# Scores of a linear attention: two heads on the two row halves of the TensorE array, their stacks filled by transfers within SBUF

## The reference, cut to what matters

```python
q = (hidden_states @ Wq).reshape(b, l, h, f).transpose(0, 2, 1, 3)   # h = 16 heads, f = 16
k = (hidden_states @ Wk).reshape(b, l, h, f).transpose(0, 2, 1, 3)
v = (hidden_states @ Wv).reshape(b, l, h, hd).transpose(0, 2, 1, 3)  # hd = 8
q = q * f ** (-0.5)
...
A = jnp.einsum('bhcf,bhsf->bhcs', qi, ki) ** 2 * mask                # within a chunk of 64
o = (inter_o + intra_o) / (inter_z + intra_z + EPS)[..., None]       # inter: all earlier chunks
...
x = x + 0.5 * ffn(layernorm(x)); x = x + attn(layernorm(x)); x = x + 0.5 * ffn(layernorm(x))
```

## Time and profile before

| | before |
|---|---|
| median of 3 runs | 235.53 us (234.33 to 237.14) |
| span of the profiled execution | 232.5 us, 6133 instructions |
| PE busy, weight loads busy | 200.5 us (86%), 161.8 us (70%) |
| DVE, ACT, POOL busy | 156.7 us (67%), 150.9 us (65%), 79.2 us (34%) |
| chain that ended last | PE 51%, DVE 30%, ACT 6%, issue 5%, DMA 5%, SP's queue 1% |

### The profile page before, as it was taken

How to read it: one execution, slowest core, us unless ns; L and a number is a source line. 1 busy time by engine, 2 the same in 40 slices (tenths; PEclk the granted TensorE clock), 3 DMA queues, 4 the chain that set the end, 5 groups by cost and what they waited for, 6 DMA issues and landing times.

```text
span 232.5 us, 6133 instructions
## 1 busy us (share of the span) xinstructions
PE 200.5 (86%) x2375; PEld 161.8 (70%) x2375; DVE 156.7 (67%) x419; ACT 150.9 (65%) x346; POOL 79.2 (34%) x100
## 2 busy tenths in 40 slices
PE   7655877849999996996999999987898999999973
PEld 7644367739798885574666567655567988899963
DVE  3878997883976792689654663869677767474162
ACT  3131596943657563865987887876899689594650
POOL 7163059994000001535445455564651000000000
PEclk9857799997999997999999999999999999999999
DMA  5996000000000599438293977936000000001103
GB/s 150 274 344 210 0 0 3 1 3 0 0 3 3 180 181 177 143 96 136 83 192 95 208 233 115 174 94 89 1 3 0 3 3 0 3 0 48 48 3 90
DMA packets 31853, 19.69 MB, mean 85 GB/s; under 512 B 1576, under 2 KB 30800, under 8 KB 31824
## 3 DMA queue, kind: packets, MB, share of 16 engines
q1 hardware_dynamic: 31824, 19.30, 35.6%
HBM read 14.05 MB, written 5.24 MB: 83 GB/s over the span
## 4 chain that ended last, share of the span: by engine, by line
PE 51%; DVE 30%; ACT 6%; issue 5%; DMA 5%; SPq 1%; POOL 0%; DVEq 0%; ACTq 0%
PE psY L873 10%; DVE xn L622 5%; PE psY L948 5%; PE psS L927 4%; PE psM L770 3%; DVE oh L690 3%; PE psM L842 3%; DVE xf L633 3%; DMA stack<-qk_parts 2%; PE psS L760 2%; PE psM L804 2%; PE psS L762 2%; PE psS L761 2%; PE psM L882 2%; DVE stats L611 2%
## 5 line engine op out<-in xcount | busy, mean ns | idle before, releaser
L492 POOL TENSOR_SCALAR_AFFINE_SELECT amat<-amat 128x512 f32<-128x512 f32 x64 | 44.8, 703 | 75.8 <-ACT amat L559 74.2
L559 ACT ACTIVATE amat<-psS 128x768 f32<-128x768 f32 x64 | 49.7, 812 | 11.9 <-PE psS L928 11.7
L530 ACT ACTIVATE hid<-psS,biasT 128x160 f32<-128x160 f32 x128 | 40.0, 399 | 10.7 <-PE psS L762 10.4
L873 PE MATMUL psY<-hid,w 128*128 128x160 f32 x256 | 41.2, 305 | 0.0
L873 PEld LDWEIGHTS psY<-hid,w 128*128 128x128 f32 x256 | 35.9, 190 | 0.4
L927 PE MATMUL psS<-stack 128*128 128x256 f16 x128 | 26.9, 277 | 2.6 <-DMA stack<-qk_parts 2.2
L760 PE MATMUL psS<-xe,w 128*128 128x160 f16 x128 | 27.8, 235 | 0.7 <-ACT xe L307 0.7
L762 PE MATMUL psS<-xe,w 128*128 128x160 f16 x128 | 27.9, 236 | 0.0
L761 PE MATMUL psS<-xe,w 128*128 128x160 f16 x128 | 27.9, 236 | 0.0
L928 PE MATMUL psS<-stack 128*128 128x128 f16 x128 | 24.2, 222 | 0.0
L948 PE MATMUL psY<-amat,vst 128*32 128x256 f32 x256 | 20.6, 391 | 1.3 <-issue 0.5
(11 more groups left out here) (138 smaller groups left out, 411.5 us busy)
## 6 DMA issues: line engine op xcount, KB each, us to landing
stack<-qk_parts SPq DMA_DIRECT2D x24, 256.0 KB, 4.5
qk_parts<-qk SPq DMA_DIRECT2D x16, 256.0 KB, 2.1
amat<-in_L_ffn_W SPq DMA_DIRECT2D x8, 256.0 KB, 6.2
w<-in_L_ffn_W SPq DMA_DIRECT2D x8, 256.0 KB, 6.2
stack<-qk_parts SPq DMA_DIRECT2D x16, 128.0 KB, 5.6
x<-in_L_attn_hidden_states SPq DMA_DIRECT2D x4, 256.0 KB, 3.3
out<-x SPq DMA_DIRECT2D x8, 128.0 KB, 1.9
amat<-in_L_attn_Wq SPq DMA_DIRECT2D x1, 128.0 KB, 3.3
```

Of the source, the lines that this page charges most:

```text
L492: pool.affine_select(out=d, in_=d, pattern=[[0, 2], [0, 2], [1, P]], compare_op=ALU.is_ge, fill=0.0, base=0, channel_multiplier=-1).then_i ...
L530: ins = act.activation(hid[:, n % 2, c, :], psS[:, 2 * (n % 2) + c // 2, (c % 2) * GS:(c % 2 + 1) * GS], ACT.Relu, bias=biasT[:, e * HC + ...
L559: act.activation(amat[:, n % A_RING, :, :], psS[:, 2 * (n % 2):2 * (n % 2) + 2, 0:T + P], ACT.Square)\
L873: ins = mm(psY[:, n % 2, 0:GS], w2[:, e, c, :], hid[:, n % 2, c, :], start=(c == 0), stop=(c == HC - 1))
```

## The change

The DRAM tensor is gone. A stack of a batch now holds eight heads on partitions 0 to 63 and the eight others on partitions 64 to 127, so that it has half the columns and no zero rows. A score pair takes one head of each half: its four matmuls contract over 64 rows each, two on the upper and two on the lower half of the array's rows, in the order half 0 and half 1 of 256 columns, then half 0 and half 1 of 128. The heads are paired as before. The weights' columns are permuted so that a q/k projection of 128 columns holds the eight heads of one half.

SP fills a batch's stack with 16 transfers from `qk16`, each from 128 partitions of 512 bytes into 16 partitions of 4096 bytes (64 KB), for each half, factor and group. `qk16` becomes a ring of two pairs; ScalarE waits, before it overwrites one, until the loads of the pair two before have landed. GpSimd no longer sets stack to zero. The weight splits of ScalarE and GpSimd are made per half, so there are four instructions where there were two.

```diff
+HALF = HEADS // 2
+ROWS = 4 * F
+LOADS = 16
...
-        qk16 = sb("qk16", [P, 2, 2, 2, PT], f16)
-        stack = sb("stack", [P, 2, 2, HEADS, T], f16)
+        qk16 = sb("qk16", [P, 2, 2, 2, 2, PT], f16)
+        stack = sb("stack", [P, 2, 2, HALF, T], f16)
...
-        scr = nc.dram_tensor("qk_parts", [NP, 2, 2, HEADS * F, PT], f16, kind="Internal").ap()
...
+        def by_half(row, w, j):
+            return row[:, WQ[w] + j * P:WQ[w] + (j + 1) * P].rearrange("p (f a c) -> p f a c", f=F, c=2)
+        def from_heads(w, j):
+            return wsml[:, WQ[w]:WQ[w] + 256].rearrange("p (a j c f) -> p j f a c", j=2, c=2, f=F)[:, j]
+        def in_half(pair):
+            return 4 * (pair // 4) + 2 * (pair % 2) + (pair % 4) // 2
...  SP
-                if s[0] == "qk":
-                    _, p, w, c = s
-                    wait_taken(sp, s)
-                    sp.dma_start(scr[p, w, :, c * P:(c + 1) * P, :].rearrange("a r t -> r a t"),
-                                 qk16[:, w, c, :, :]).then_inc(qk_stored[2 * w + c], 16)
-                elif s[0] == "ld":
+                if s[0] == "ld":
                     b = s[1]
                     p = b // 2
-                    for c in range(4):
-                        sp.wait_ge(qk_stored[c], 16 * (p + 1))
+                    for w in range(2):
+                        for j in range(2):
+                            wait_taken(sp, ("qk", p, w, j))
                     if b >= 2:
                         sp.wait_ge(s_ready, (b - 1) * HEADS // 2)
-                    for w, r, part, np_ in ((0, 0, 0, 2), (0, 2, 0, 2), (1, 0, 0, 2), (1, 2, 1, 1), (1, 3, 0, 1)):
-                        src = scr[p, w, part:part + np_, :, (b % 2) * T:(b % 2 + 1) * T].rearrange("a (f h) t -> (a f) h t", f=F)
-                        sp.dma_start(stack[r * F:(r + np_) * F, b % 2, w, :, :], src).then_inc(stack_loaded[b % 2], 16)
+                    for j in range(2):
+                        for w in range(2):
+                            for r in range(4):
+                                part = r % 2 if w == 0 or r < 2 else 1 - r % 2
+                                lo = ROWS * j + r * F
+                                src = qk16[:, p % 2, w, j, part, (b % 2) * T:(b % 2 + 1) * T]
+                                sp.dma_start(stack[lo:lo + F, b % 2, w, :, :], src).then_inc(stack_loaded[b % 2], 16)
...  GpSimd
-            link(pool.memset(stack[4 * F:, :, :, :, :], 0.0))
             link(pool.memset(vst[:, :, :, :, :], 0.0))
...  ScalarE
-                    if p:
-                        act.wait_ge(qk_stored[2 * w + c], 16 * p)
-                    act.activation(qk16[:, w, c, 0, :], bank(s), ACT.Copy, scale=F ** -0.5 if w == 0 else 1.0)\
+                    if p >= 2:
+                        for par in range(2):
+                            act.wait_ge(stack_loaded[par], LOADS * 16 * (p - 1))
+                    act.activation(qk16[:, p % 2, w, c, 0, :], bank(s), ACT.Copy, scale=F ** -0.5 if w == 0 else 1.0)\
...
                     for w in range(2):
-                        o = WQ[w]
-                        act.activation(wsm[:, 0, o:o + 256].rearrange("p (f h) -> p f h", h=HEADS),
-                                       wsml[:, o:o + 256].rearrange("p (h f) -> p f h", f=F), ACT.Copy)
+                        for j in range(2):
+                            act.activation(by_half(wsm[:, 0, :], w, j), from_heads(w, j), ACT.Copy)
...  TensorE
-                        pe.wait_ge(stack_loaded[b % 2], 5 * 16 * (b // 2 + 1))
-                        if b == 0:
-                            pe.wait_ge(zeros_made, 2)
+                        pe.wait_ge(stack_loaded[b % 2], LOADS * 16 * (b // 2 + 1))
...
-                    for j in range(2):
-                        h = HEAD_ORDER[2 * pair + j]
-                        d = psS[:, 2 * (n % 2) + j, :]
-                        q, k = stack[:, b % 2, 0, h, :], stack[:, b % 2, 1, h, :]
-                        mm(d[:, P:P + T], k[:, 0:P], q, start=True, stop=True)
-                        ins = mm(d[:, 0:P], k[:, P:T], q[:, P:T], start=True, stop=True)
+                    h = in_half(pair)
+                    for st in range(TT):
+                        for j in range(2):
+                            rows = slice(ROWS * j, ROWS * (j + 1))
+                            d = psS[:, 2 * (n % 2) + j, :]
+                            q, k = stack[rows, b % 2, 0, h, :], stack[rows, b % 2, 1, h, :]
+                            if st == 0:
+                                mm(d[:, P:P + T], k[:, 0:P], q, start=True, stop=True)
+                            else:
+                                ins = mm(d[:, 0:P], k[:, P:T], q[:, P:T], start=True, stop=True)
```

More of the change, by code:

```diff
@@ L281, in macaron_program @@
         qk_hi = sem("qk_hi")
-        qk_stored = [sem(f"qk_stored{c}") for c in range(4)]
         stack_loaded = [sem(f"stack_loaded{c}") for c in range(2)]
@@ L474, in _ @@
             for w in range(2):
-                o = WQ[w]
-                pool.tensor_tensor(wsm[:, 1, o:o + 256].rearrange("p (f h) -> p f h", h=HEADS),
-                                   wsml[:, o:o + 256].rearrange("p (h f) -> p f h", f=F),
-                                   wsm[:, 0, o:o + 256].rearrange("p (f h) -> p f h", h=HEADS), ALU.subtract)
+                for j in range(2):
+                    pool.tensor_tensor(by_half(wsm[:, 1, :], w, j), from_heads(w, j), by_half(wsm[:, 0, :], w, j), ALU.subtract)
             pool.tensor_tensor(wsm[:, 1, WV:], wsml[:, WV:], wsm[:, 0, WV:], ALU.subtract).then_inc(wsm_split, 1)
             pool.wait_ge(wsm_split, 2)
-            link(pool.memset(stack[4 * F:, :, :, :, :], 0.0))
             link(pool.memset(vst[:, :, :, :, :], 0.0))
@@ L731, in _ @@
                     dve.wait_ge(qk_hi, n + 1)
-                    dve.scalar_tensor_tensor(out=qk16[:, w, c, 1, :], in0=bank(s), scalar=F ** -0.5 if w == 0 else 1.0,
-                                             in1=qk16[:, w, c, 0, :], op0=ALU.mult, op1=ALU.subtract).then_inc(taken(s), 1)
+                    dve.scalar_tensor_tensor(out=qk16[:, p % 2, w, c, 1, :], in0=bank(s), scalar=F ** -0.5 if w == 0 else 1.0,
+                                             in1=qk16[:, p % 2, w, c, 0, :], op0=ALU.mult, op1=ALU.subtract).then_inc(taken(s), 1)
                 elif kind == "ox":
```

## The result

| | before | after |
|---|---|---|
| median of 4 runs each | 235.09 us (234.33 to 237.14) | 239.48 us (238.45 to 240.87) |
| ratio, 95% interval | | 1.0178 (1.012 to 1.0236) |
| profiled execution: time, span | span 232.5 us | 238.45 us, span 236.6 us |

The change makes the kernel 1.8% slower.

What follows compares the result with a forecast made beforehand. It took the kernel to be mostly a queue of TensorE work (86% busy) with holes in it. The terms -4.3 - 0.5 + 0.2 - 1.0 = -5.6 us took 235.5 to 229.9, stated as 230.0, range 223.5 to 238.5.

Steps and rivals of the forecast that it cites:

- The memset: Before the attention: dropping GpSimd's zeroing of stack frees a VectorE cast and TensorE's idle behind it, -4.3 us.
- The first load: Entry of the attention: stall ahead of the first score 1.8 us instead of 2.25, so -0.5 us.
- T: Time of one batch's stack load, first issue to the end of its landing: 10.3 us, bounds 8.3 to 12.2.
- The transport: Moving a load's 1.05 MB into 16 partitions per transfer: 8.7 us at an assumed 120 GB/s.
- The later loads: Loads inside the attention: they fit between batches, with a small stall at batch 5, +0.2 us.
- The supply becomes the bound: Rival: issues of 0.67 us or under 100 GB/s, T = 13, stalls in the attention, 238.4 us; chance 0.1.
- ScalarE's new wait: Ahead of the third and fourth pairs' qk evictions, for loads of two pairs before: at most some 0.5 us.
- The scores: Attention: two halves side by side save 9.9 us, array-shape switches cost 8.3; 0.6 of the net counts, -1.0 us.
- The borders: Switches of array shape around runs of scores: 0.09 us entering, 0.2 leaving, 0.05 more into value matmuls; 8.3 us.
- Switches are free: Rival: changes between full and half rows cost nothing, about 225.6 us; chance 0.2.

Runs made afterwards that it cites:

- e1: The kernel before with only the zeroing memset split into 16 GpSimd instructions: 230.08 us, 0.9757 of before.
- m1: The changed kernel with 48 extra 64 KB test transfers on SP before the attention, eight of each of six forms: one run, 240.61 us.
- e4: The changed kernel with q and k side by side, so a batch's load is eight transfers of 128 KB, not sixteen of 64: 230.27 us, 0.9783 of before.
- e5: The changed kernel with 4 of each batch's 16 load transfers issued by GpSimd instead of SP: 231.43 us, 0.9871 of before.
- e12: The kernel before's full-array scores over 128 rows with zeros, stacks through DRAM by rows, memset in 16 pieces: 232.47 us, 0.9917 of before.
- e14: e8 with each of the two load transfers waiting only for its own stores: 229.73 us, 0.9781 of before.
- e8: The changed kernel's scores on halves, but stacks stored to DRAM by rows and loaded by two transfers into 128 partitions: 229.03 us, 0.9718 of before.
- e9: e8 with a pair's four matmuls ordered half 0, half 0, half 1, half 1: 229.09 us, 0.9828 of before.
- e16: The changed kernel with each four load transfers waiting only for their own qk eviction, not all four: 234.17 us, 0.9961 of before.

## Why the prediction was wrong, step by step

**The memset** was right in mechanism: -4.3 forecast, -4.6 read from the trace of after, -5.6 (3.7 to 7.8 by its interval) as a change alone in e1.

**The first load is the step that failed**, in the sentence "The new patterns are plain on both sides, so nearer 0.41". The price of an issue stood between two rows, 0.366 for stores and 0.627 for loads, and I chose by the look of the pattern. m1 shows that plain patterns do not help: it is 0.60 for a transfer within SBUF in all three of them, so 0.645 a start instead of 0.41, and with one longer issue in most loads T = 12.3 to 13.3 instead of 10.3. The transport, to which I gave the term, was not the limit. As a sum it was right, 10.3 against the 10.0 of e4's undisturbed loads, by two errors that cancel: 7.5 us of moving for 8.7, and 1.3 behind the last packet for 0.4. The landing of 2.1 was 2.3. The forecast of the stall was 1.8 us, at most 3.7 by its bound; it was 4.08.

**The later loads** follow from the same T: 6.2 us of stalls instead of 0.2. The rival *The supply becomes the bound* had this nearly to the letter, T = 13 and 238.4 us for the 239.48 measured, four stalls of 4.5, 1.6, 2.7 and 1.4 us, for which it names no batches, against 4.08, 2.00, 2.33 and 1.20 at batches 0, 3, 5 and 7, and two small ones more. Some luck is in that: by the prediction's own sum issues of 0.67 us give T = 12.2, and what makes it 13 are the single longer issues, which it did not have. It should not have had 0.1: its condition, 0.67 us an issue, was a number that stood in the earlier trace rows, and e4 and e5 each take its cost back nearly whole. "Supply" was the right word; of its two conditions the issue held and the rate did not. ScalarE's new wait was 2.8 us once, not 0.5.

**The scores** were right in their pair (0.175) and in their sum, by two errors that cancel. The borders were too dear: the entries cost 0.095, as worked out, the exits to full-array work the same and not 0.2, and the exits to the value matmuls nothing new, so 57 borders make 5.4 us and not 8.3, and the net on TensorE is 4.5, not 1.6. But the share of it that counts, 0.6 by the earlier trace rows, is 0.4 for the overlap, roughly: e12 and e14 are 1.5 us apart, for the 1.0 forecast. In after itself, first to last score without the 6.2 us of stalls is 83.66 us against 84.16, 0.5 less. So the size is right within what single traces tell, no more. The rival *Switches are free* falls.

**The sum** with what was measured: -4.6 for the memset, +1.8 at the first score, +6.2 of later stalls, -0.5 for the scores: +2.9, where I had -5.6; with the +1.0 at the span's head and +0.1 behind the attention it is the +4.1 of the spans up to rounding. Between the medians it is +4.4. The range ended at 238.5, just above the 238.4 of the supply rival, whose terms also add up to +2.9. The microsecond by which 239.48 lies outside is of the size of the +1.0 at the head of the span, which is variation; that the forecast of 230.0 lies 9.5 us too low is the price of an issue.

## What to carry to other kernels

Count the issues of a stage, not its bytes: many small transfers within SBUF are a queue of their own on SP, 0.64 us each here, and are a limit as soon as they come near the time of the stage that they feed. When an unknown price lies between two rows, and one of them carries the kernel over to slower, the range and the chances have to be made from that row. And a change that bundles a gain (a memset that held another engine's cast) with a cost hides that the gain can be had alone, here with three lines and 2.4%.

## What the runs showed of the hardware

- A transfer of 64 KB within SBUF keeps SP's queue for 0.60 us in three patterns of partitions, one from or to a contiguous block of DRAM for 0.43 (m1); loads from rearranged DRAM keep it for 0.63 and 0.66 (e8). GpSimd issues one within SBUF in 0.53 (e5).
- A switch between 128-row and 64-row matmuls costs TensorE 0.095 us each way; from 64 rows to the column quarters it costs no more than from 128 rows.
- TensorE's records show two row halves starting 0.006 us apart even where the program has them one behind the other (e9).
- One GpSimd memset held a 64-element VectorE cast for its whole rest, 4.5 us; in pieces of 0.9 us, for 0.8.
- TensorE's granted clock behind an idle stretch is not told by that stretch's length: ahead of the first score it was idle 4.08 us in after, 2.25 in before and 1.97 in e4, and the 3.5 us behind were at 0.54, 0.51 and 0.76; but behind 3.70 us in e12, 2.77 in e14 and 1.34 in e16 they were at 1.00. A window of before, for comparison with the two of e16's section, and e12's:

```profile
88.80:92.30 3.50, 3.33 (x17) 2.74 (x18) 0.81 (x2) 1.70 (x3) 0.64 (x1) 0.51 1.24 197
```

```profile
85.93:89.43 3.50, 3.49 (x28) 2.45 (x29) 1.38 (x2) 2.60 (x5) 1.03 (x2) 1.00 1.13 186
```
